# Order of issue in the causal attention stages: all four score products of a group first, the division of the preceding group ahead of the maxima

## The reference, cut to what matters

```python
q, k = _rope(q, k)
k = jnp.repeat(k, g, axis=2)        # g = 4
v = jnp.repeat(v, g, axis=2)
scores = jnp.einsum('bqhd,bkhd->bhqk', q, k) / np.float32(np.sqrt(HEAD_DIM))
causal = jnp.tril(jnp.ones((S, S), bool))
scores = jnp.where(causal[None, None], scores, jnp.float32(-1e+30))
attn = jax.nn.softmax(scores, -1)
o = jnp.einsum('bhqk,bkhd->bqhd', attn, v).reshape(B, S, NHEADS * HEAD_DIM)
x = x + o @ wo
```

## Time and profile before

| | us |
|---|---|
| runs | 3690.25, 3679.31, 3684.36 |
| median | 3684.36 |
| span of the profiled execution | 3687.3 |
| PE busy | 3303.7 (90% of the span) |
| DVE busy | 2631.0 (71%) |
| ACT busy | 1933.5 (52%) |
| POOL busy | 990.3 (27%) |

### The profile page before, as it was taken

The page is one execution under the profiler, slowest core; times in us unless marked ns, Lnnn a source line. Parts: engine busy times, 40 slices in busy tenths (PEclk is TensorE's granted clock), DMA queues, the critical chain, the costliest instruction groups (busy, mean ns, idle before and its releaser), DMA issues. The chain is left out here.

```text
span 3687.3 us, 65201 instructions
## 1 busy us (share of the span) xinstructions
PE 3303.7 (90%) x22154; PEld 2194.8 (60%) x22154; DVE 2631.0 (71%) x8703; ACT 1933.5 (52%) x5275; POOL 990.3 (27%) x960
## 2 busy tenths in 40 slices
PE   6999999987997899997899999988799749999975
PEld 4666767664554344445667667665455437887853
DVE  5888888885444788873788888887344567777755
ACT  4667767664222366774676767666222125555531
POOL 3211112233454001012121212143444332222213
PEclk8999999998998689997999999998899769999986
DMA  4140500013755322302060500011756300000010
GB/s 129 52 170 7 166 1 1 20 48 110 178 91 116 70 46 58 73 23 72 1 220 1 172 1 1 4 48 57 215 88 122 89 1 15 1 16 4 1 34 23
DMA packets 202239, 234.78 MB, mean 64 GB/s; under 512 B 20662, under 2 KB 188536, under 8 KB 201080
## 3 DMA queue, kind: packets, MB, share of 16 engines
q1 hardware_dynamic: 170968, 190.48, 17.0%
q0 software_dynamic: 30944, 40.14, 6.5%
HBM read 98.13 MB, written 133.73 MB: 63 GB/s over the span
## 5 line engine op out<-in xcount | busy, mean ns | idle before, releaser
L1816 ACT ACTIVATE p_prob<-bank,p_small 128x256 f32<-128x256 f32 (+3 forms) x1280 | 646.2, 515 | 156.0 <-DVE p_small L1988 151.3
L1988 DVE CUSTOM_DVE_ANT_0 bank<-bank,p_mask 128x256 f32<-128x256 f32 (+3 forms) x1280 | 579.0, 490 | 97.1 <-PE bank L1559 85.7
L2336 POOL TENSOR_TENSOR p_tm<-p_rope_a,p_rope_b 128x512 f32<-128x512 f32 x192 | 245.8, 1280 | 1269.0 <-DVE p_rope_b L1968 1264.5
L1559 PE MATMUL bank<-p_k,p_q 64*128 64x256 f32 (+3 forms) x3840 | 529.2, 347 | 13.6 <-ACT p_prob L1816 12.5
L1821 ACT ACTIVATE p_prT<-bank 128x512 f32<-128x512 f32 x752 | 426.0, 601 | 211.5 <-PE bank L1568 209.6
L1568 PE MATMUL bank<-g_ident,p_prob 128*128 128x128 f32 x3008 | 438.3, 284 | 54.4 <-DVE p_prob L1997 20.8
L1997 DVE TENSOR_SCALAR p_prob<-p_prob,p_small 128x256 f32<-128x256 f32 (+3 forms) x1280 | 424.5, 395 | 11.3
L1577 PE MATMUL bank<-p_prT,p_v 128*64 128x512 f32 (+1 forms) x1504 | 428.2, 619 | 0.3 <-ACT p_prT L1821 0.3
L1568 PEld LDWEIGHTS bank<-g_ident,p_prob 128*128 128x128 f32 x3008 | 330.0, 142 | 150.6 <-issue 50.2
L1559 PEld LDWEIGHTS bank<-p_k,p_q 64*128 64x128 f32 (+1 forms) x3840 | 339.1, 188 | 116.1 <-issue 65.1
L2034 DVE TENSOR_REDUCE p_nmax<-bank 128x1 f32<-128x512 f32 x512 | 320.8, 683 | 56.8 <-PE bank L1618 54.6
(11 more groups left out here) (288 smaller groups left out, 6215.8 us busy)
## 6 DMA issues: line engine op xcount, KB each, us to landing
sorted<-p_blank SPq DMA_DIRECT2D x32, 2304.0 KB, 19.2
p_w<-in_L_ffn_w SPq DMA_DIRECT2D x96, 256.0 KB, 4.5
p_h_in<-sorted SPq DMA_DIRECT2D x158, 144.0 KB, 2.7
p_k_st<-k_saved SPq DMA_DIRECT2D x16, 288.0 KB
p_q_st<-q_saved SPq DMA_DIRECT2D x16, 288.0 KB
g_stage<-in_L_ffn_wq SPq DMA_DIRECT2D x8, 512.0 KB, 3.8
g_stage<-in_L_ffn_wo SPq DMA_DIRECT2D x16, 256.0 KB, 4.3
q_saved<-p_qp SPq DMA_DIRECT2D x16, 256.0 KB, 3.2
```

The source lines that it names most:

```text
L1559: ins = pe.matmul(h.use.ap[:, 0:n], q[rows, at, :], k[rows, kp, o.g, keys], start=i == 0, stop=i == 2)
L1816: act.activation(s.prob.ap[:, 0:s.o.w], s.use.ap[:, 0:s.o.w], ACT.Exp, bias=sm[:, 0, j:j + 1], scale=-1.0, accum_out=sm[:, 1, j:j + 1]).th ...
L1988: dve.tensor_tensor_reduce(x, x, A.mask[:, A.mask.shape[1] - o.w:], -1.0, FAR, ALU.add, ALU.min, o.sm.ap[:, 0, h.j:h.j + 1]).then_inc(made)
```

## The change

The steps of the causal stages are issued in another order; no instruction is added, removed or altered. Before, a step issued: scores of heads 0 and 1; value product; division of the preceding group; piece 1; exponentials of heads 0 and 1; low part; projection; piece 2; scores of heads 2 and 3; two turns; exponentials of heads 2 and 3; piece 3; the other turns; piece 4. After, it issues: division of the preceding group; scores of all four heads; exponentials of all four; value product; piece 1; low part; projection; piece 2; two turns; piece 3; the other turns; piece 4. For the windowed attention (`wide`) the order is as it was.

```diff
                 cur = group(c, b, unit, t, g)
                 nturn = prev.nkt if prev else 0
-                scores(cur, *((0,) if wide else (0, 1)))
-                weighed = weigh(full) if full else None
-                if prev:
-                    normalise(prev)
-                route_last()
-                beside()
-                exponentials()
+                if wide:
+                    scores(cur, 0)
+                    weighed = weigh(full) if full else None
+                    if prev:
+                        normalise(prev)
+                    beside()
+                    exponentials()
+                else:
+                    if prev:
+                        normalise(prev)
+                    scores(cur, 0, 1)
+                    scores(cur, 2, 3)
+                    exponentials()
+                    weighed = weigh(full) if full else None
+                    route_last()
+                    beside()
                 if weighed:
                     weighed = low_parts(weighed)
                 if wide:
...
                 route_last()
                 beside()
-                if not wide:
-                    scores(cur, 2, 3)
                 route_last()
                 for kt in range(0, min(2, nturn)):
                     turn(prev, kt)
-                exponentials()
                 if wide:
+                    exponentials()
                     scores(cur, 2)
                 beside()
                 if wide and weighed:
...
                 for kt in range(2, nturn):
                     turn(prev, kt)
                 route_last()
-                exponentials()
                 if wide:
+                    exponentials()
                     scores(cur, 3)
                     exponentials()
                 beside()
```

## The result

Slower by more than forecast: 4016.3 us in the median of 4 runs (4012.6 to 4018.1), against 3686.8 (3679.3 to 3690.3) for the kernel before on the same chip. The ratio is 1.0899, 95% interval 1.0881 to 1.0916: 330 us more, where I had forecast 229 and given 3785 to 4050 as the range. The profiled execution has a span of 4013.6 us and a mean granted clock of 0.92. Of that span PE is busy for 82%, DVE 68%, ACT 48%, POOL 25%.

The account below looks back on a forecast made before the run. PE's nearly full queue was taken as the bound. 30 units at 7.3 us (219) plus 10 for first units made 229 us more: 3916 on the profiled span, 3913 on the median (chance 0.57), range 3785 to 4050.

Parts of the forecast that it names:

- The bound: Steady causal stages: PE's queue, over 99% busy, limits the kernel; one bank wait of 0.37 us a unit; reordering gains little.
- The banks of the scores: PE's scores of heads 2 and 3, moved forward: their banks are already free, so they cost what they did.
- The chain and its tail: Second turn waits for alternating DVE and ACT work; DVE idles for ACT's last exponential and copy, about 1.45 us a step.
- the table's 49.2 + 7.3: Per causal unit: 49.2 us before, 7.3 longer: 6.8 from DVE and ACT waits, 0.4 to 0.5 in (0, 0).
- The division: DVE's division, moved ahead of the maxima, at its old prices: 1.27 us for 256 wide, 1.5 for 384, 1.88 for 512.
- The clock: Rival, chance 0.16: PE's 2.3 us idle in (2, 0) also lowers the clock, 5 us a unit, 150 more, 4063 us.
- The count: Both causal stages: 30 x 7.3 = 219 us, plus 4 x 2.5 = 10 for first units; last unit at nothing.
- The marks: Signs of being right: PE about 87% busy, unit about 56.5 us, 200 us waiting for named DVE lines, wide stage unchanged.
- the marks of "wrong": Signs of error, steady stretches: PE at 98% or more, turns waiting for DVE line 1997 instead, or clock below 0.95.
- Half the price: Rival, chance 0.14: DVE's idle time per step is partly hidden, 0.75 us instead of 1.45; 3787 us.
- Faster: Rival, chance 0.08: PE's waits do not grow; the 0.36 us wait goes, scores as one block save 26 us; 3646.
- no change: Rival, chance 0.05: only a small loss and gain, +4 us, or DVE gets ahead further than reckoned; 3688 us.

Follow-up runs that it names:

- the kernel with the sums held: Kernel after, with POOL's two sums of the rotated queries and keys held until the next step's division is made: 3917.4 us, ratio 1.0627.
- the last run on PE's part: Kernel before, with only PE's scores of heads 2 and 3 moved forward and DVE's low part ahead of piece 1: 3951.1 us, ratio 1.0715.

## Why the forecast was right in kind and short in size

**The bound** was read rightly: PE's queue was full, order could only lose, and the low part ahead of the first piece shows that even its last visible wait was worth nothing.

**The banks of the scores** "cost what they did": true in the main of the change as a whole (the turns' waits dominate; PE waits for an exponential only 8.6 us from 200 to 700 us), but only because the exponentials moved forward with them, as the 3915.6 us of the scores alone show. Issued as one block they even cost less, 1.59 us for four of 512 (601.93 to 603.52) instead of twice 0.89 or 0.90. PE's queue gains 0.2 us a step by that and waits as much longer for DVE's chain, which the forecast's idle times left out.

**The chain and its tail**, the main term: confirmed in place and size. The tail was forecast as 1.43 to 1.5 us and 2.0 in (3, 1); the rows have 1.37 and, in the kernel with the sums held, 1.39 in (3, 0) and 1.88 in (3, 1). Taking it away (exponentials behind the copies) gave back 171 us. With the sums held a unit at full clock takes 56.5 us, as the table's 49.2 + 7.3 says; with a fall of the clock in it, it takes 57.2 to 57.9, and the ten steady units of the first stage have a mean of 57.1:

```profile
526.22:582.74 56.52, 47.03 (x339) 34.09 (x337) 40.73 (x147) 34.01 (x100) 8.06 (x9) 1.00 0.00 1
582.74:640.05 57.31, 48.46 (x338) 34.88 (x336) 41.53 (x141) 36.22 (x102) 12.99 (x10) 0.97 0.00 1
```

**The division**, the term that failed. The prediction took "a division: 1.27 for 256 wide, 1.88 for 512, between them 1.5 for 384, below 1.1 for 128" from a row in which POOL had nothing to do beside it, and moved it to a place just behind the rotation, where POOL's sums run. It counted DVE's and ACT's instructions at the new place, but not who else is at work there. Four division instructions behind a rotation take 1.99 us at 128, 2.26 at 256 and 2.60 at 384. Where no sums run beside them they take 0.87 (514.28 in the kernel before), 1.14 and 1.41 (584.52 in the kernel after). The steps (1, 0), (2, 0) and (3, 0) each have one such division on DVE's chain: 1.12 + 1.12 + 1.19 = 3.4 us a unit.

**The clock**, a rival with 0.16, came, at less than a third of its price. From 200 to 700 us the turns wait for query low 16 times, 53.1 us in all, which is 8 x (3.68 + 2.97): every unit has both of these idle times. Only the longer one goes with a fall. At 1.2 GHz PE then spends about 7 us in most units (mean clock 0.94) and half of that in the others (0.97). Where it costs can be read in the step (2, 1) behind the wait that ends at 583.79. There the value product takes 2.95 us at the lower clock instead of 1.94 (535.50 in the kernel before), and the tail grows:

```profile
590.68 0.69 DVE L2009 TENSOR_TENSOR p_oT_lo<-bank,p_oT_hi 128x512 fp32r<-128x512 f32 x1 [2.32 <-ACT p_oT_hi L1832]
```

In the unit at full clock of the kernel with the sums held this wait is 1.37 us. DVE also waits 0.27 us for scores and 0.25 for products in this step, and not at all there: 0.95 + 0.27 + 0.25 = 1.5 us in all. The lengths agree: a short fall costs 0.8 us (57.3 against 56.5 above), a long one about 0.7 more (61.54 against 60.80). The rival had 5 us, because it took 13 us at the lower clock. With 3.4 and 1.5 the unit of 56.5 becomes 61.4; 61.5 was measured. No kernel was run to change the clock alone; besides these rows, the two kinds of unit in the last run on PE's part differ in the clock and take 1.5 us more where it falls.

```profile
434.61:495.41 60.80, 48.61 (x338) 34.41 (x336) 46.84 (x148) 34.05 (x100) 10.25 (x11) 0.97 0.77 256
557.21:618.81 61.60, 49.38 (x338) 35.45 (x336) 45.30 (x145) 34.05 (x100) 8.21 (x8) 0.94 0.00 1
```

**The count.** 14 units of the first stage take 878.1 us (from 122.60 to 1000.70) instead of 720.8: 11.2 each. The ten steady ones lose 12.2 on average, the first and the last three, which are longer in both kernels, 5 to 11, in place of the forecast 7.3 and 7.3 + 2.5. What stands ahead of them, costed at nothing, is 9.3 us longer; why wasn't looked into. In the second stage the fourteen lose 159.8 us, and 12.8 are lost between the two. What follows came out 13.0 us shorter, with no change in it; it is 12 us shorter in the kernel before with the low part first as well, so this is scatter. Together 326 us, the difference of the two spans.

**The marks.** Named as right: PE's share near 87% (80% came), 56.5 us a unit (61.5), 200 us of waiting for the named lines (316 in the three rows above), query low and the low part waiting for ACT's copies (both), the wide stage unchanged (yes). Of the marks of "wrong", one came to its edge: a clock of 0.95 in the steady stretches. That 4016 still lies inside the range owes something to luck: the upper end, 4050, was put there for a dearer fall of the clock, and the division's wait, which took up part of that room, was in no term and no rival.

**The rivals.** "Half the price" fell: the tail is there in full. "Faster" and "no change" fell with it. The rule of the Trainium skill ("Perfetto Trace Analysis", Optimization Strategy) that pointed at the ring agrees with the trace in the place: PE's waits in the steady part are waits for a bank, and with one bank for the turns the kernel takes 284 us more. No run has more banks, so whether the ring is too short in itself isn't shown; taking the tail and the collision away gave back 243 us with the same ring.

Why does the division suffer and the maxima beside the same sums do not? The Trainium skill, "SBUF — State Buffer", section Who interferes with whom, has a rule of that kind: in some performance modes a vector operation with a scalar uses both of VectorE's ports into SBUF, of which it shares one pair with GpSimd. Whoever issues first has that pair for its whole instruction, and the other waits. An instruction with at most one input from SBUF and outside these modes doesn't contend. The traces agree. A piece of the division that finds GpSimd's operation running ends 0.15 to 0.3 us behind it, whether that lasts 0.87 or 3.78 us; the maxima, which read their scores from PSUM, suffer nothing. And where a piece of the division was first, GpSimd's operation is the longer one: 0.87 us for 256 columns instead of 0.73 (530.88 in the kernel before), and 3.78 for the weights' 1536 instead of 3.48 (559.01 there). In which mode the division runs is told by no trace.

## What to carry to other kernels

A price read from a trace holds for the place where it was read: before moving an instruction, list what every other engine, those with a low busy share as well, does at the new place. In strict queues, four quick maxima and exponentials issued as a block delay everything behind them on both engines, and a ring of buffers passes that delay on to the engine that was full. And when an order is tuned, test its parts in pairs: each half of this change made the kernel slower, for the most part for another reason than the whole.

## What was unexpected of the hardware

A VectorE division of f32 by a per-partition scalar does not share time with GpSimd's addition or subtraction of two f32 tiles. A piece that meets one running ends 0.15 to 0.3 us behind it: 0.99 us instead of 0.34 beside a 128x512 addition, 3.70 instead of 0.48 beside a subtraction of 3.78 us. Four pieces of 256 columns so take 2.26 to 2.73 us instead of 1.14. VectorE's maxima of PSUM beside the same addition keep their time (0.57 us for 384, with POOL's sums from 529.46 to 531.61 in the kernel before). On PE an idle time of 2.56 us, in the kernel with the sums held, left the mean clock of its unit (526.22 to 582.74) at 1.00, though the next unit had 0.97; in the kernel after, with 3.68 us, PE was granted 1.2 GHz next. In the last run on PE's part the clock fell in 16 of 20 steady units, and in the one looked at (531.13 to 589.45) the waits just ahead of the fall are of 0.69 and 0.93 us.
